# GpSimd fetches new and old cache rows by turns instead of in two batches of three

## The reference, cut to what matters

```
x = x + attention(x)              # paged KV cache, window of 256 positions, 8 query and 4 key heads of 64
x = x + x_b @ L1_weights[subject_b]          # a matrix along the tokens, chosen by sequence
x = x + base2(x) + lora2(x, adapter2_b)      # rank 16, chosen by sequence
x = x + base3(x) + lora3(x, adapter3_b)      # rank 16, chosen by sequence
```

```
k_blocks = k_blocks.at[blk, :, off, :].set(k)
v_blocks = v_blocks.at[blk, :, off, :].set(v)
k_all, v_all = k_blocks[block_tables], v_blocks[block_tables]
p = softmax(where(kpos <= pos and kpos > pos - 256, q @ k_all / 16, -inf))
o = p @ v_all ;  out = o @ Wo
```

## Time and profile before

| | |
|---|---|
| median of 3 runs | 442.44 us (441.16 to 442.81) |
| span of the profiled execution | 494.4 us; no other time is given for it |
| PE busy | 444.6 us, 90% of the span |
| DVE busy | 311.1 us, 63% |
| POOL busy | 268.9 us, 54% |
| ACT busy | 230.2 us, 47% |

### The profile page before, as it was taken

The page is one execution under the profiler, slowest core; times in us unless marked ns, Lnnn a source line. Parts: engine busy times, 40 slices in busy tenths (PEclk is TensorE's granted clock), DMA queues, the critical chain, the costliest instruction groups (busy, mean ns, idle before and its releaser), DMA issues.

```text
span 494.4 us, 9866 instructions
## 1 busy us (share of the span) xinstructions
PE 444.6 (90%) x2890; PEld 320.9 (65%) x2890; DVE 311.1 (63%) x901; ACT 230.2 (47%) x590; POOL 268.9 (54%) x241
## 2 busy tenths in 40 slices
PE   5999999996898999989799989897979898989997
PEld 2434468453666777767577767685858675767776
DVE  4988885682646666747465757565647565666543
ACT  1322113653445555646355646554445554555541
POOL 2598157487364756555546556556555556554000
PEclk9999999999799999999989999999999999999999
DMA  6396859755346544453434445353534453434111
GB/s 199 109 302 197 296 170 288 271 144 167 85 110 179 141 115 143 115 147 99 136 100 142 113 143 129 111 147 106 149 88 122 123 141 82 123 104 109 47 54 44
DMA packets 76266, 69.08 MB, mean 140 GB/s; under 512 B 50516, under 2 KB 52692, under 8 KB 76214
## 3 DMA queue, kind: packets, MB, share of 16 engines
q1 hardware_dynamic: 57248, 42.03, 28.7%
q0 software_dynamic: 15456, 22.08, 16.5%
q10 hardware_dynamic: 3510, 4.35, 2.4%
HBM read 78.39 MB, written 11.93 MB: 183 GB/s over the span
## 4 chain that ended last, share of the span: by engine, by line
PE 71%; DVE 11%; issue 9%; ACT 4%; another core or an unknown queue 3%; DMA 2%; ACTq 0%; DVEq 0%; SPq 0%
PE banks L1112 27%; PE banks L1244 8%; PE banks L1125 7%; PE banks L1279 7%; PE banks L1252 5%; PE banks L1106 5%; PE banks L1264 5%; DVE prob L974 3%; DVE x L887 2%; PE banks L1226 2%; ACT x L662 2%; PE banks L1292 2%; DMA kvb<-kvl_dram 1%; PE banks L1378 1%
## 5 line engine op out<-in xcount | busy, mean ns | idle before, releaser
L514 POOL DMA_INDIRECT windows<-kvrows_dram,idx_all x78 | 82.6, 1059 | 63.7 <-PE banks L1264 29.0
L634 ACT ACTIVATE pt_s<-banks 112x384 f32<-112x384 f32 x128 | 57.7, 498 | 96.5 <-PE banks L1252 70.9
L514 POOL DMA_INDIRECT windows<-newkv,idx_all x78 | 79.4, 1019 | 27.6 <-issue 22.4
L974 DVE CUSTOM_DVE_ANT_0 prob<-banks,mask 128x336 f32<-128x336 f32 x128 | 58.5, 505 | 52.1 <-issue 22.4
L628 ACT ACTIVATE prob<-prob,negmax 128x336 f32<-128x336 f32 x128 | 72.4, 567 | 32.3 <-DVE negmax L974 18.3
L484 POOL TENSOR_TENSOR rstd<-ms,half 128x8 f32<-128x8 f32 x24 | 45.9, 1913 | 66.4 <-DVE ms L907 46.2
L1125 PE MATMUL banks<-wkv_s,xt_s 128*128 128x512 f32 x128 | 58.7, 616 | 5.6 <-DMA xt_s<-xt_dram 5.6
L1252 PE MATMUL banks<-cst,prob 128*112 128x128 f32 x384 | 52.7, 273 | 0.2
L1264 PE MATMUL banks<-pt_s,windows 112*64 112x128 f32 x624 | 41.8, 281 | 10.6 <-ACT pt_s L634 8.7
L1112 PE MATMUL banks<-wf_hi,x 128*128 128x512 f32 x120 | 41.7, 408 | 10.5 <-DVE x L887 10.5
L1244 PE MATMUL banks<-kt_s,qt_s 64*128 64x336 f32 x256 | 47.5, 471 | 2.8 <-issue 2.8
(11 more groups left out here) (212 smaller groups left out, 825.0 us busy)
## 6 DMA issues: line engine op xcount, KB each, us to landing
usel<-utab SPq DMA_DIRECT2D x64, 128.0 KB
xt_s<-xt_dram SPq DMA_DIRECT2D x31, 256.0 KB
newkv<-kvo SPq DMA_DIRECT2D x16, 256.0 KB
stage<-xtok_dram SPq DMA_DIRECT2D x16, 256.0 KB
tsel<-ttab SPq DMA_DIRECT2D x64, 64.0 KB
out_dram<-xo ACTq DMA_DIRECT2D x15, 256.0 KB
windows<-kvrows_dram,idx_all POOLq DMA_INDIRECT x78
windows<-newkv,idx_all POOLq DMA_INDIRECT x78
```

The costliest lines, as they stand in the source:

```text
L514: P.indirect_dma_start(kv_s[i][:, c, :], None, newkv if new else kvrows, bass.IndirectOffsetOnAxis(ap=idx_all[:, new * CH + c, b:b + 1], a ...
L634: A.activation(pt_s[g][:], tb[g % 2][0:KP, 0:CH * 128].rearrange("p (c q) -> p c q", c=CH), ACT.Copy).then_inc(S["pt_ev"], 1)
L974: V.tensor_tensor_reduce(out=prob[b % 3][:, g, :], in0=sbk[g][:, 0:WK], in1=mask[b % 2][:], scale=-1.0 / 16, scalar=3.0e38, op0=ALU.add, o ...
```

## The change

`gather` is cut into a helper `piece` that issues one of the three transfers. In the passes from 1 on, the wait for `pv_mm >= k` moves to the front, then comes the wait for the old rows of window `k + 2`, and then the transfers go out by turns: new chunk 0 of window `k + 2`, old chunk 0 of window `k + 4`, new chunk 1, old chunk 1, new chunk 2, old chunk 2. The number of transfers, their sizes, their targets and their semaphores stay as they are. `root_query` stays last in the pass. Passes 28 and 29 issue new chunks alone, without the wait for `pv_mm`, as before.

```diff
+            def piece(b, new, c):
+                i = b % WINDOWS
+                P.indirect_dma_start(
+                    kv_s[i][:, c, :], None, newkv if new else kvrows,
+                    bass.IndirectOffsetOnAxis(ap=idx_all[:, new * CH + c, b:b + 1], axis=0),
+                    bounds_check=NB * NT if new else NPOOL * BLOCK - 1, oob_is_err=False,
+                ).then_inc(kv_in[i], 16)
+
             def gather(b, new):
-                i = b % WINDOWS
                 if new:
-                    pool.wait_ge(kv_in[i], 96 * (b // WINDOWS) + 48)
+                    pool.wait_ge(kv_in[b % WINDOWS], 96 * (b // WINDOWS) + 48)
                 for c in range(CH):
-                    P.indirect_dma_start(
...
+                    piece(b, new, c)
...
-                if k + 2 < NB:
-                    gather(k + 2, 1)
                 if k + 4 < NB:
                     pool.wait_ge(S["pv_mm"], k)
-                    gather(k + 4, 0)
+                if k + 2 < NB:
+                    pool.wait_ge(kv_in[(k + 2) % WINDOWS], 96 * ((k + 2) // WINDOWS) + 48)
+                    for c in range(CH):
+                        piece(k + 2, 1, c)
+                        if k + 4 < NB:
+                            piece(k + 4, 0, c)
                 if k % 2 == 0 and k // 2 + 1 < TILES:
                     root_query(k // 2 + 1)
```

## The result

The changed kernel takes 447.38 us (median of 4 runs, 447.23 to 449.46), the kernel before 442.26 us (4 runs beside it). The ratio is 1.0116, 95% interval 1.008 to 1.0153: **slower by 1.2%**, 5.1 us. A second comparison of the same two kernels gave 1.0115 (1.0081 to 1.0148). The forecast was no change at 442.4 us; the measured time lies inside the range of 438.5 to 449.0, but on the side that had 0.18 of the chance.

What follows compares the result with a forecast made beforehand. TensorE, busy 90% of the span, was taken as the bound, with GpSimd costing time only where others wait for it. Five steps of 0 us each left the median at 442.4 us; range 438.5 to 449.

Steps and rivals of the forecast that it cites:

- Step 1: GpSimd's power in even passes, now behind six fetches: `rstd` still 0.47 us early for `query_last` in pass 8; cost 0.
- Step 2: GpSimd's successive blocks: neither delays the next one's start, 2.6 us to spare before the even block; cost 0.
- Step 3: New rows landing before TensorE's key transposes: 5.3 us available, landing estimated near 2 to 3 us; cost 0.
- Rival B: New rows land late and TensorE waits 1 us in some 13 passes: slower, 455 us; chance 0.04.
- Step 4: Old rows on GpSimd: last fetch starts 3.87 us later, but its new rows are asked for some 23 us later; cost 0.
- Step 5: VectorE beside GpSimd: moved fetches avoid its copies and scalings; counted 0, bounds 0 and -2.5 us.
- rival C: Less disturbance halves the excess in VectorE's odd-pass maxima waits (22.4 us in all): faster, 438.7 us; chance 0.13.
- rival A: Power comes late in even passes 2 to 26: slower, 450.0 us paid in full, +2.2 less cover; chance 0.14.

Runs made afterwards that it cites:

- move_alone: Kernel before with the wait for `pv_mm` moved to the front, then three new and three old fetches as two batches, without turns; ratio 1.0017.
- old_first: Kernel before with the wait for `pv_mm` moved to the front, then the three old fetches, then the three new ones; ratio 1.0283, 455.44 us.
- power_before_last_old: Changed kernel with the power of even passes one fetch earlier, ahead of the last old fetch; ratio 1.0123 to the kernel before.
- new_one_pass_ahead: Turns as in the changed kernel, but new rows of window `k + 3` instead of `k + 2`; ratio 1.1358 to the kernel before, 502.17 us.

## Why the prediction was wrong

**Step 1, the power: right.** It starts right behind the sixth fetch, and is in time by 0.97 us in pass 8 (0.47 forecast; the power took 1.68 us instead of 2.04). It is late in pass 18 alone, behind the pause of 2.33 us, which no row of before had shown; this costs about 1.0 us (`move_alone`). Moving the power forward did not take the loss away (1.0123).

**Step 2, the blocks: right in cost, wrong in its picture.** The blocks do not delay each other. But the arrival of `pv_mm` was read from an execution with a tile period of 24 us. At 20.6 us GpSimd did not wait for `pv_mm` before the change at all to speak of; now it waits 1.9 to 2.0 us for it in nearly every pass (about 3.5 us forecast for the odd ones).

**Step 3, the landing: this is the step that failed.** "I take a value near 2 to 3 us" and "even the upper bound fits with 0.1 us to spare". The cover was as forecast in even passes: from the end of the last new fetch to the key transposes lie 5.5 us in an undisturbed one (191.60 to 197.12 in the changed kernel; 5.3 forecast). In odd passes it is 5.9 us, not 7.7. The landing is the term that was sized wrong. It takes 4.1 to 6.4 us, median 4.9, and goes over the cover in five windows. The 5.24 us that I took for an upper bound came from one wait in the start of the kernel, behind other loads, and was near the usual value. The low end would have been right for a queue left to itself: without `usel` loads the median is 2.3 us. But the reason for choosing it, that the start was crowded and new rows are few, left out what sets the time, namely SyncE's `usel` loads, beside which two of the 16 shares come late. The working never asked what else moves at the moment when the rows land.

**Rival B was the case, with 0.04 of the chance.** Its place was right, its cause only in part: it let the new rows queue behind the old ones, and without old rows the loss does go (1.0020), but the median landing of even windows stays at 5.2 us; the long part is the tail behind the `usel` loads. Its price was not right either: not 1 us in each of 13 passes (455 us) but 0.4 to 2.5 us in five, 4.6 us in one profile. That `old_first` comes to 455.4 us is luck: there all 13 even windows do wait, but they fall back by 0.1 to 3.8 us each, and half clock adds to it. **Step 4** is right. **Step 5 and rival C**: the maxima's waits without a named cause, 22.4 us in the earlier trace rows, belonged to that one long execution; they are 2.8 us in the second profile of before and 2.7 us after the change, and there was nothing to gain from them.

**What was right by chance.** The sum was made on an execution 12% longer than the runs. I noted the 52 us and used them for rival A alone. The right use was to distrust each margin read from it. That step 1 and the even cover came out close is partly luck, since both intervals were read from passes 12% longer. What made that execution long is not shown.

## What to carry to other kernels

A transfer that is asked for later is judged by its landing time at that very place, and a bound taken from one wait elsewhere is a sample, not a ceiling; where the margin left is a few tenths of a microsecond, give the case that it breaks a real chance. Gathered rows land with their slowest share, so a load of another queue that fills only two of the transfer engines can hold them up while the engines look idle on average. Here it was enough to put 16 rows outermost in place of two copies. Put what the next engine waits for at the front of a block, and what nobody waits for behind it.

## What the runs showed of the hardware that I had not expected

- Less traffic did not make it faster: without the `tsel` loads the changed order took 450.3 us against 446.7, and the `usel` loads went out in one row. That this is the cause is not shown.
- Spreading the same bytes by another outermost dimension took `old_first` from 455.44 to 442.53 us. Of the 16 shares of a gather, two came a median of 2.0 us late in the changed kernel beside the unspread loads, and 0.2 us beside the spread ones.
- A single wait of 2.6 or 3.2 us was followed by 6.8 us at a granted clock of 0.50 (`old_first`, `power_before_last_old`). So a wait can cost more than its length.
- GpSimd pauses once in the loop for 2.2 to 2.4 us behind one fetch (pass 18), at the same place in every kernel with the moved wait but `new_one_pass_ahead`. In the changed kernel one 8 KB packet of the profile's queue for instructions (q14) lies inside the pause, at 291.8 of 290.2 to 292.5 us, and so it is in eight other profiles; in the kernel before, one comes at 289.7, just ahead of 2.16 us in which GpSimd waits for `ms` anyway. So the loading of instructions is the likely cause, and before, the wait for `ms` would have hidden it; no run changes the loading alone, so it is not shown.
- One execution of the kernel before had a span of 494.4 us, another 440.1 us, with the same median of runs. The long one has three stretches at half clock in its loop, 13.7 us together, which explain at most 7 of the 54 us.
